# A feature-interaction tower on one core: the whole kernel rebuilt (x1 inside x2's slots, B tiles by matmul, more one-hot rows, spaced gathers, last output in two parts)

## The reference

```python
Xk = X0                                  # X0 = e
for W in (W0, W1, W2):                   # each gives 64 rows of 16
    Xk = jnp.einsum('bfd,bhd,fho->bod', X0, Xk, W.reshape(F_, H_prev, 64))
    outs.append(Xk.sum(axis=2))
h = jnp.concatenate([z, dense_ctx], axis=1)      # 192 + 16
h = jnp.maximum(h @ W_top1 + b_top1, 0.0)        # 512
h = jnp.maximum(h @ W_top2 + b_top2, 0.0)        # 256
y = h @ W_top3
```

## Time and profile before

| | |
|---|---|
| median of 3 runs | 558.97 us (556.06 to 561.19) |
| span of the profiled execution | 555.2 us, 3.8 us under that median |
| mean granted TensorE clock | 0.822 of full |
| DMA bytes | 85.82 MB, mean 155 GB/s |
| VectorE busy in products | 225.0 + 57.6 us, 240 products |
| GpSimd busy in gathers | 189.1 + 34.1 us, 176 gathers |

### The profile page before, as it was taken

The page is one execution under the profiler, slowest core; times in us unless marked ns, Lnnn a source line. Parts: engine busy times, 40 slices in busy tenths (PEclk is TensorE's granted clock), DMA queues, the critical chain, the costliest instruction groups (busy, mean ns, idle before and its releaser), DMA issues.

```text
span 555.2 us, 6844 instructions
## 1 busy us (share of the span) xinstructions
PE 376.4 (68%) x2332; PEld 169.9 (31%) x2332; DVE 311.6 (56%) x295; ACT 156.7 (28%) x333; POOL 233.6 (42%) x187
## 2 busy tenths in 40 slices
PE   3567467772919386592929485784939493949987
PEld 3454211220304033241414133331414141414445
DVE  2523274672929283764929292846648392939730
ACT  0121021312314051332324060423323242414242
POOL 5874067757840786038820787048810000000000
PEclk9686778795968779696978879696969787887999
DMA  5655969897978888796979878787969697873400
GB/s 133 180 142 117 228 124 209 154 250 125 210 143 186 178 164 171 133 186 120 207 133 197 163 161 185 153 172 152 184 132 192 139 201 147 192 157 63 96 0 1
DMA packets 79666, 85.82 MB, mean 155 GB/s; under 512 B 48679, under 2 KB 51895, under 8 KB 79644
## 3 DMA queue, kind: packets, MB, share of 16 engines
q1 hardware_dynamic: 65628, 81.95, 69.7%
q0 software_dynamic: 5680, 1.55, 3.2%
q10 hardware_dynamic: 8336, 2.02, 1.7%
HBM read 49.83 MB, written 2.10 MB: 94 GB/s over the span
## 4 chain that ended last, share of the span: by engine, by line
SPq 39%; DMA 29%; PE 22%; issue 4%; ACT 4%; DVE 1%; ACTq 0%
SPq L276 30%; DMA A<-x_scratch 19%; PE ps_x L447 16%; SPq L256 5%; DMA small_sb<-small_tables 4%; PE ps_x2r L493 3%; PE ps_tower L447 2%; DMA x_scratch<-x_small 2%; SPq L283 2%; DMA B<-x_sb 2%; ACT x_sb L688 1%; ACT x_sb L683 1%; SPq L261 1%; DMA x_scratch<-x_cols 1%; PE ps_g L447 1%
## 5 line engine op out<-in xcount | busy, mean ns | idle before, releaser
L409 DVE TENSOR_TENSOR Z<-A,B 128x1024 f32<-128x1024 f32 x192 | 225.0, 1221 | 44.5 <-DMA B<-x_sb 32.5
L214 POOL DMA_INDIRECT x_rows<-tbl,ids_tile x144 | 189.1, 1313 | 46.9 <-issue 42.0
L447 PE MATMUL ps_x<-Z,w_sb 128*64 128x512 f32 x768 | 190.3, 615 | 19.0 <-DVE Z L409 18.6
L401 DVE TENSOR_TENSOR Z<-A,C 128x1024 f32<-128x1024 f32 x48 | 57.6, 1223 | 158.8 <-ACT A L667 137.7
L493 PE MATMUL ps_x2r<-id_sb,x_sb 128*128 128x128 f32 x64 | 16.9, 416 | 126.0 <-ACT x_sb L688 126.0
L667 ACT COPY A<-A 64x1024 f32<-64x1024 f32 x32 | 33.4, 1042 | 209.0 <-DMA A<-x_scratch 208.9
L447 PEld LDWEIGHTS ps_x<-Z,w_sb 128*64 128x64 f32 x768 | 50.1, 140 | 105.4 <-issue 81.0
L447 PE MATMUL ps_x<-Z,w0s_sb 128*64 128x512 f32 x192 | 73.4, 919 | 9.5 <-DVE Z L401 9.5
L228 POOL COPY ids_tile<-ids_sb 128x24 int32 x6 | 9.5, 1580 | 110.4 <-PE ps_x L454 110.4
L493 PEld LDWEIGHTS ps_x2r<-id_sb,x_sb 128*128 128x128 f32 x64 | 10.8, 207 | 141.6 <-ACT x_sb L688 140.8
L702 ACT ACTIVATE x_diag<-ps_x,mask_sb 128x192 f32<-128x192 f32 x128 | 50.7, 613 | 2.9 <-PE ps_x L503 2.9
(11 more groups left out here) (47 smaller groups left out, 166.9 us busy)
## 6 DMA issues: line engine op xcount, KB each, us to landing
B<-x_sb SPq DMA_DIRECT2D x128, 256.0 KB, 6.2
C<-x_scratch SPq DMA_DIRECT2D x46, 512.0 KB, 7.8
A<-x_scratch SPq DMA_DIRECT2D x32, 256.0 KB
A<-x_scratch SPq DMA_DIRECT2D x16, 512.0 KB, 8.3
x_rows<-tbl,ids_tile POOLq DMA_INDIRECT x144
x_unit<-x_scratch SPq DMA_DIRECT2D x16, 128.0 KB
x_scratch<-x_cols ACTq DMA_DIRECT2D x14, 96.0 KB
C<-x_scratch SPq DMA_DIRECT2D x4, 256.0 KB
```

The lines of the kernel that those rows point to most:

```text
L214: pool.indirect_dma_start(out=x0_rows[:, f * D:(f + 1) * D], out_offset=None, in_=tables[f], in_offset=bass.IndirectOffsetOnAxis(ap=ids_of ...
L401: nc.vector.tensor_tensor(by_q(Z[r]), by_d(A[e][i]), by_d(C[i]), ALU.mult)\
L409: nc.vector.tensor_tensor(by_q(Z[r]), by_d(A[e][i]), by_q(B[e][j]), ALU.mult)\
L447: return nc.tensor.matmul(out, lhsT, rhs, start=start, stop=stop)
```

## The change

Nearly all of the kernel is written anew. What it does:

- **Order.** In unit u's slot the next unit's three x1 products come before x2's product 6 in the first two units (`FIRST`) and first of all from then on. x2's products go by B first (n = 3j + i).
- **A and C.** A is loaded whole, three loads of 512 KB per unit into a ring of three sets; C is two loads of 512 KB into two sets, and ScalarE makes the third from them (`copy_c`, two copies of 64x1024). Unit 1's loads are issued once unit 0's second C has landed.
- **B.** B lies in PSUM, in two double banks. TensorE makes all four (`make_b`: x1 times a 0/1 matrix) for units 0 to 3 (`PB`), and the first one until unit 13 (`LB`). The others come by DMA (two loads of 256 KB each) into SBUF and ScalarE copies them to PSUM (`copy_b`, 128x1024). Units 14 and 15 take the first B by DMA and use it from SBUF.
- **x0.** The scratch is [tile, field, row, column]; a tile is stored straight from the gathered rows by one DMA on SyncE's queue in runs of 64 bytes (`store_rows`, 3072 for a tile); there is no transpose and no copy. x0_unit becomes a load of 96 KB in runs of 1 KB. Products and copies have plain layouts.
- **One-hot rows.** Also tile 1's first set of 8 fields is made by one-hot matmuls: 26 steps of 128 table rows in place of 18. The ids of two sets are spread over partitions by a matmul with ones. Tile 1 needs 16 gathers.
- **Gathers.** Before each gather from tile 1 on, GpSimd writes 144 columns of a scratch (memset), waits for it, and waits for a count of products that spaces a tile's 24 gathers over two slots. Row buffers are doubled. Loops on all engines are unrolled.
- **Dense layers.** Weights are cut into halves of 64 columns. The last group runs in two parts: three units' rows first, then the last unit's.

```diff
+PAUSE = 144
+AS = 3
+MADE = ((0, 0), (0, 1), (1, 0))
+FIRST = (6, 6)
+PB = 4
+LB = 14
...
+            for t in range(1, TILES):
+                if t >= 2:
+                    wait_stored(pool, t - 2)
+                for n, f in enumerate(gathered_fields(t)):
+                    pool.memset(pause_sb[:, :], 0.0).then_inc(paused, 1)
+                    pool.wait_ge(paused, gathers(t - 1) + n + 1)
+                    after(pool, z_ready, PER_SLOT * (2 * t - 5) + 2 * PER_SLOT * f // F)
+                    gather(t, f, gathered[t % 2])
...
+        def store_rows(queue, t, fs, stored):
+            v = x0_dram[t:t + 1, fs, :].rearrange("t f (b d) -> (t b) f d", d=D)
+            src = x0_rows[t % 2][:, D * fs.start:D * fs.stop].rearrange("p (f d) -> p f d", d=D)
+            queue.dma_start(v, src).then_inc(stored, 16)
...
+            def load_b(u, k):
+                j = k + 1
+                if k == 0:
+                    sp.wait_ge(x1_copied, u + 1)
+                if u > PB:
+                    sp.wait_ge(b_copied, (NJ - 1) * (u - 1 - PB) + k + 1)
+                for q in range(2):
+                    src = x1_sb[u % 2][H * q + j:H * (q + 1):NJ, :].unsqueeze(1)
+                    sp.dma_start(B_sb[k][:, HALF * q:HALF * (q + 1)], src.to_broadcast([HR, FR, HALF]))\
+                        .then_inc(b_in[k], 16)
...
+            for u in range(2, UNITS):
+                if u == 2:
+                    store_tile(1)
+                if u % 2 == 0:
+                    wait_stored(sp, u // 2)
+                sp.wait_ge(z_ready, made_x1(u - 2, NI - 1))
+                for i in range(NI - 1):
+                    load_c(u, i)
+                for i in range(NI):
+                    if u >= AS:
+                        sp.wait_ge(z_ready, made_x2(u - AS, NP2 - NI + i))
+                    load_a(u, i)
+                if u > LB:
+                    load_b0(u - 1)
+                if u > PB:
+                    for k in range(NJ - 1):
+                        load_b(u - 1, k)
+                if u % 2 == 1 and u + 1 < UNITS:
+                    store_tile((u + 1) // 2)
+                sp.wait_ge(x0_turned, u - 1)
+                load_quarters(u)
...
+                nc.vector.tensor_tensor(Z[s % ZR][:, :], A[u % AS][i][:, :],
+                                        B0_sb if u >= LB and j == 0 else ps_b[j % 2][:, :], ALU.mult)\
+                    .then_inc(z_ready, 1)
...
+            def make_b(u, j):
...
+                for q in range(2):
+                    m = mm(ps_b[j % 2][:, HALF * q:HALF * (q + 1)], pick_sb[H * q:H * (q + 1), j, :],
+                           x1_sb[u % 2][H * q:H * (q + 1), :])
+                m.then_inc(b_made, 1)
...
+                for n in range(NP2):
+                    if n == x1_at(u) and u + 1 < UNITS:
+                        for i in range(NI):
+                            cross1(u + 1, i)
...
+            def copy_b(u, k):
+                act.wait_ge(b_in[k], 32 * (u - PB + 1))
+                if k > 0:
+                    act.wait_ge(z_ready, made_x2(u, NI * k - 1))
+                else:
+                    act.wait_ge(z_ready, made_x2(u - 1, NP2 - 1))
+                nc.scalar.copy(ps_b[(k + 1) % 2][:, :], B_sb[k][:, :]).then_inc(b_copied, 1)
```

More of the change, by code:

```diff
@@ L209, in _, with gather @@
         def _(pool):
-            pool.dma_start(ids_sb[:, :], ids).then_inc(ids_in, 16)
             pool.wait_ge(ids_in, 16)
-            def gather(ids_of, f):
+            def gather(t, f, landed):
                 pool.indirect_dma_start(
[L215 to L228, removed]
-                pool.wait_ge(ids_ready, t - 1)
-                pool.sem_inc(gathers_begun, 1)
-                for f in range(F):
-                    gather(ids_tile, f)
+                    out=x0_rows[t % 2][:, f * D:(f + 1) * D], out_offset=None, in_=tables[f],
@@ L354, in _ @@
+            load_b0(UNITS - 1)
+            for k in range(NJ - 1):
+                load_b(UNITS - 1, k)
             sp.wait_ge(y_ready, GROUPS)
@@ new lines, in last_h1 @@
+            def last_h1(part, m, bank):
+                g = GROUPS - 1
+                if m == 0:
+                    pe.wait_ge(z12_ready, 4 * g + 4 + part)
+                    pe.wait_ge(z3_ready, 2 * (g + part + 1))
+                if part == 1:
+                    pe.wait_ge(h1_ready, M1 // 128 * g + m + 1)
+                for k, (weights, rows) in enumerate(((wt1a_sb, z1_dense), (wt1b_sb, z23))):
+                    for e in range(2):
+                        at = 128 * m + 64 * e
+                        last = mm(of_part(bank[64 * e:64 * (e + 1), 0:GROWS], part), weights[:, at:at + 64],
+                                  of_part(rows[:, :], part), k == 0, k == 1)
+                last.then_inc(h1_summed, 1)
@@ L636, in _ @@
-            sum_y(GROUPS - 1)
+                cross1(0, i)
+                keep_warm(WARM[1 + i])
+            pe.wait_ge(pick_in, 16)
+            make_b(0, 0)
+            make_b(0, 1)
+            pe.wait_ge(w1_in, 16)
+            pe.wait_ge(diag_fixed, 1)
+            for u in range(UNITS):
+                slot(u)
+            last_z3(0, ps_tower, range(F // 4))
+            turn_x2(UNITS - 1)
+            last_z3(0, ps_tower, range(F // 4, F // 2))
+            sum_g(UNITS - 1, 0)
+            sum_g(UNITS - 1, 1, ps_x1)
@@ new lines, in slot, with copy_ids @@
+                if PB <= u + 1 < UNITS:
+                    copy_b(u + 1, 0)
+                if x1_at(u) > 0 and x1_at(u + 1) == 0:
+                    copy_c(u + 2)
+            act.wait_ge(mask_in, 16)
+            nc.scalar.copy(first_sb[:, :], mask_sb[:, :])
+            def copy_ids(m):
+                for half in range(2):
+                    act.wait_ge(ids_spread, 2 * (m - 1) + half + 1)
+                    nc.scalar.copy(small_ids_f32[m][:, IDS // 2 * half:IDS // 2 * (half + 1)], spread_bank(m, half)[:, :])\
+                        .then_inc(ids_copied, 1)
@@ new lines, in _ @@
+            copy_c(0)
+            copy_x1(0)
+            copy_c(1)
+            for u in range(UNITS):
+                slot(u)
+            last_z1()
+            last_z2(0)
+            copy_x2(UNITS - 1)
+            copy_x2_rows(UNITS - 1)
+            last_copy_z3(0, ps_tower)
+            copy_g(UNITS - 1, 0)
+            copy_g(UNITS - 1, 1, ps_x1)
+            last_z2(1)
+            last_relu_h1(0, 0)
+            last_copy_z3(1, ps_tower)
+            for m in range(1, M1 // 128):
+                last_relu_h1(0, m)
@@ L850 @@
     order = by_size[SETS * FR:] + sets[0] + sets[1]
[L851 to L853 removed]
+    cr = 128
+    chunks = [-(-max(rows[f] for f in fs) // cr) for fs in sets]
     small_tables = np.zeros((FR, sum(chunks) * cr, D), np.float32)
```

879 lines of the change are left out of this document (451 added, 428 removed).

## The result

The changed kernel takes **374.61 us** (median of 4 runs, 372.82 to 376.53) against 557.51 us of the kernel before (554.47 to 561.19) beside it: a ratio of 0.675 [0.670, 0.680]. Forecast was 394 in a range of 358 to 440.

What follows compares the result with a forecast made beforehand. The prediction took DMA loads in SyncE's queue as the bound. Start 43, three slots of 19.5, nine of 22.5, slots 12 to 15 and a tail of 13 made 390, plus 3.8 outside the span: 394 us, range 358 to 440.

Steps and rivals of the forecast that it cites:

- first rival: Slots 3 to 11: engines set the pace at 19.3 us a slot, 364 us in all; chance 0.18.
- the likeliest case: Slots 3 to 11: transfers set the pace at 22.5 us a slot, 394 us in all; chance 0.50.
- the loads' sum: Slots 3 to 11: loads, quarters, store, gathers and B's wait add up to 22.5 us a slot.
- quarters: Slots 3 to 11: the quarters' load in 1 KB runs costs 0.4 us a slot.
- store: Slots 3 to 11: a tile's 64-byte runs in SyncE's queue cost 6.0 us a tile, 3.0 a slot.
- gathers: Slots 3 to 11: GpSimd's gathers add 1.1 us a slot to the transfers.
- B's wait in the queue: Slots 3 to 11: SyncE's queue waits for B's SBUF tile to be free, 0.5 us a slot.
- TensorE's and VectorE's terms: Per slot: TensorE 19.0 us, 19.5 with waits at turns; VectorE 18.2 us, its products at 1.15 to 1.22.
- the rival in which PSUM halves the rate: VectorE's products: the PSUM operand halves their rate, 33.8 us a slot, near 596 in all; chance 0.04.
- GpSimd's term: Gathers over two slots: 39 to 41 us a tile against 39 to 45 available, so just covered.
- its rival: Gathers stay at 1.97 us beside every product, 62 us a tile, so GpSimd sets the pace: 504 us; chance 0.05.
- The forecast's 13 us: Tail after slot 15: about 13 us against 19.4 before, as part of the last dense layers runs earlier.

Runs made afterwards that it cites:

- experiment 3: Changed kernel with TensorE making all of B in every unit, no B load by DMA: 413.6 us, ratio 0.737.
- experiment 4: Changed kernel with the stores of tiles 1 to 7 in runs of 1536 bytes in place of 64: 370.01 us, ratio 0.659.
- experiment 2: Changed kernel with B's first quarter also loaded by DMA from unit 4 on, ten fewer make_b: 392.23 us, ratio 0.696.
- experiment 9: Kernel before with three gathers a tile in place of 24 from tile 2 on: 572.06 us, ratio 0.988.
- experiment 1: Changed kernel with B copied from 16 adjacent rows of x1 in place of every fourth of 64: 374.41 us, ratio 0.665.
- 6: Changed kernel without the memset before a gather and the wait for a count of products: 372.95 us, ratio 0.666.
- 10: Kernel before with its x0_unit load in runs of 1 KB in place of 64 bytes: 571.74 us, ratio 0.990.
- 11: Kernel before with SyncE's loop over tiles unrolled, nothing else changed: 577.04 us, ratio 0.994.
- experiment 5: Changed kernel with products of B's loaded quarters reading SBUF directly from unit 4 on, without ScalarE's copies: 383.33 us, ratio 0.684.
- experiment 7: Changed kernel with the last group of the dense layers in one part after the last product: 376.06 us, ratio 0.671.

## Why the prediction was right, and where it was not

**Right in kind and size of gain, within its range; the pace in slots 3 to 11 was the first rival's.** The loads did leave the path as forecast: SyncE's queue is off the chain, the A waits went from one of 7 to 9 us per unit to 7.0 us in the whole run, and 30.4 us a unit became 19.4. But the likeliest case said that transfers would bound these slots at 22.5, and the first rival that engines would at 19.3. The measured pace, 19.4, is the rival's, and so is its reason in the main: experiment 3 shows TensorE at its limit (1.03 us for each added pair), and experiment 4 leaves 19.1 us a slot when the stores' short runs go. The transfers stand just behind: their share is 0.98, and in experiment 2 17.8 of 20.6 us are paid for added bytes. So 374.61 us lies in the rival's case (350 to 380, chance 0.18) and not in the forecast's own (380 to 415, chance 0.50). That it is within the stated range is due to the range's width, which took in a part of that rival.

**The step that failed is the loads' sum of 22.5 us a slot.** The pair of slots from 139.8 to 177.9 us moved 18.8 x 254 + 19.3 x 204 = 8.71 million bytes' worth in 38.1 us. Taking the store's 6 us with 0.56 MB out, the rest ran at 254 GB/s. The forecast for a pair was 45; beside it the same sum with this trace's rates:

| term of a pair | forecast | by the trace's rates |
|---|---|---|
| loads, 8.39 MB | 35.0 at 240 GB/s | 33.0 at 254 |
| quarters | 0.8 | 0.8 |
| store | 6.0, with nothing beside | 6.0, less 1.4 for the 0.36 MB of others that move in it |
| gathers | 2.2 | inside the rate |
| B's wait in the queue | 1.0 | none seen |
| sum | 45.0 | 38.4 (38.1 measured) |

So of 6.9 us some 2.2 were gathers, which the 254 GB/s already carry (experiment 9 puts them at 0.4 us a unit even in the kernel before, not 1.1), 2.0 the rate, 1.4 the store's share and 1.0 the wait. The 6 us for a store, worked out from x0_unit's 64-byte runs, was right by the windows; that it could be hidden by two units' lead was not seen: experiment 4 puts all seven stores at 2.8 to 4.4 us.

**The rate was misread: 243 GB/s was not the most that the kernel before shows.** Its page has a slice of 14 us, 111 to 125 us, at 250, and in it B copies that stand behind queued C loads:

```profile
118.00:126.00 8.00, 4.89 (x18) 0.92 (x16) 3.88 (x4) 0.00 (x0) 6.27 (x5) 0.87 1.06 266
```

After, 182 to 186 us runs at 278, mostly B copies too. In the later B phases of the kernel before the same copies were slower:

```profile
210.00:212.00 2.00, 2.00 (x24) 1.21 (x22) 1.69 (x2) 0.00 (x0) 1.70 (x2) 1.00 0.91 165
...
214.00:216.00 2.00, 2.00 (x24) 1.14 (x22) 0.23 (x1) 0.00 (x0) 1.64 (x2) 1.00 0.83 158
```

The share is 0.83 and 0.91 for 158 and 165 GB/s (189 and 196 in the two windows beside them), so the same bytes kept the engines busy longer. Why **stays open**: neither the source rows (experiment 1), nor the gathers (6 and 9), nor x0_unit's runs (10), nor the loop (11) moved the time by more than 1.2%, and a packet of 2 KB stayed at 126 to 130 ns in experiments 1 and 6, and at 157 to 171 in 9 to 11, where the changed kernel has 126 and the kernel before 162. What differs, and was not tried by itself, is whether loads are queued ahead of the copies: they are in the fast stretch above and in the changed kernel. SyncE's slow issues alone are not the reason, as those of the fast stretch came every 1.6 us too; but with no queue ahead, eight issues of 256 KB in 12.52 us are 168 GB/s, and no run tells whether there the issues hold up the copies or the copies the issues.

**The Trainium skill's fabric ceiling** of 435 GB/s (DMA: Bandwidth & Descriptors, Specifications) was set aside in the prediction because windows with a share over 1.0 stopped at 243 GB/s. That reading was wrong, as the 266 above shows, and at the changed kernel's start, where the tables and ids are loaded, one window comes close to the ceiling:

```profile
7.00:9.00 2.00, 0.58 (x1) 0.00 (x0) 1.50 (x3) 0.59 (x1) 1.70 (x2) 1.00 1.01 400
...
280.00:282.00 2.00, 2.00 (x10) 0.70 (x12) 1.26 (x2) 1.56 (x3) 0.00 (x0) 1.00 1.06 331
```

Over a whole slot of A, B and C loads, though, the changed kernel has 254 to 256 GB/s at the most and experiment 2 has 271, with a share of 1.05 to 1.06, so the Trainium skill's ceiling is no price for a slot here. No run tells what makes these loads slower than those of the start. The rival's pace came out without that reason.

**TensorE's and VectorE's terms held.** A make_b is two halves that overlap, 1.03 us by experiment 3 and 1.06 in the chain, forecast 0.87 with 1.73 as the other end. Products from PSUM are 1211 ns, forecast 1.15 to 1.22, and the rival in which PSUM halves the rate fell. `sum_x1` took 0.68, not 1.05; its input now lies in order, which no run tried by itself. The granted clock is 1.00 in the windows, forecast 1.0; with it full, slots 0 to 2 came out 0.7 us off in 58.5.

**GpSimd's term held, and its rival fell.** The 88 gathers that lie wholly under products with B in PSUM are all 0.95 us, as in idle phases before. The rule in the Trainium skill (GPSIMD Engine Reference, the table of specifications) that two SBUF inputs of VectorE contend with GpSimd agrees with experiment 5's 1.76. But the rival's 504 us had gathers at 1.97 throughout, and experiment 5 took 383.33: there the 41 gathers wholly under products from two SBUF tensors have a mean of 1.49 us, and of the others 39 lie wholly under PSUM products and 29 in VectorE's pauses. In the kernel before the same mean was 1.90.

**The end was 9.1 us dearer than forecast** (slot 15 by 1.6, tail by 7.5), against 27.5 us saved beyond the forecast in slots 3 to 11. The forecast's 13 us was set against 19.4 before, which runs from ScalarE's copy of the last x2; the sum, however, ends slot 15 with VectorE's last product, 4.6 us ahead of that copy. Like for like, from the copy at 355.08 us, the tail is 15.9 us: 3.5 less than before and not 6, as experiment 7 shows. The other 4.6 was left out of the sum.

**Errors that cancelled:** 27.5 us too much in slots 3 to 11 and 2.1 in slots 0 to 2 and 12 to 14, 9.1 too little at the end, 1.4 at the start: 19.1 of span. The forecast of 394 is 19.4 us high.

## What to carry to other kernels

Before a price from a saturated window is added to others, ask what else was moving in that window: its rate may already hold the small traffic beside it. The best window that was looked at is a lower bound for the transfers, not a limit: look through the whole page for a faster one. When the sums of two resources lie as close as 22.5 and 19.5 us here, give the pace at which the second one binds nearly the weight of the first. A tail is to be counted from the same event as the last repeated part ends with, or a few microseconds between the engines fall through.

## What the runs showed of the hardware

- VectorE's fp32 product of 128x1024 costs the same with its second operand in PSUM (1211 ns) as in SBUF (1216 and 1221).
- GpSimd's gathers were 0.95 us under products with a PSUM operand, all 88 of them, and up to 1.76 (experiment 5) and 1.97 (before) under those from two SBUF tensors, with means of 1.49 and 1.90.
- SBUF to SBUF copies in rows of 2 KB moved 278 GB/s in the changed kernel (182 to 186 us), and in the kernel before 266 at 118 to 126 us and 158 to 196 at 208 to 216 us, at shares of 1.09, 1.06 and 0.83 to 0.91.
- The highest rate in a window of 2 us was 400 GB/s at a share of 1.01, in the loads of tables and ids; a slot of repeating loads in the changed kernel had 254 to 256 at 1.05 to 1.06.
- A store in runs of 64 bytes (192 KB) held the transfers at 73 to 131 GB/s for 6 us, and yet seven stores took only 2.8 us of time by the traces, 4.4 by the medians.
- On one chip TensorE's matmuls at the start came at some 34 to 55 records in 20 us, with no wait that the profile names, where another chip issued 128 in 6.14 us.
